# A macaron block on one core: the first feed-forward block's weights quantised by groups of output columns among its first tiles, with ScalarE's sign for part of the groups

## The reference, cut to what matters

```
def _quantize(w):
    gamma = jnp.mean(jnp.abs(w))
    return jnp.clip(jnp.round(w / (gamma + EPS)), -1.0, 1.0)

def _bitlinear(x, w):
    return jnp.matmul(x, _quantize(w).T)

x1 = _bitlinear(x, w1)                 # w1, w2: (1408, 512), w3: (512, 1408)
x2 = _bitlinear(x, w2)
hidden = jax.nn.sigmoid(x1) * x2
return _bitlinear(hidden, w3)
```

## Time and profile before

| | us |
|---|---|
| median of 3 runs | 2888.96 (2887.87 to 2891.6) |
| profiled execution, its span | 2888.6 |
| TensorE busy in the span | 2796.3 (97%) |
| VectorE, ScalarE, GpSimd busy | 2294.6, 1626.3, 1363.4 |

### The profile page before, as it was taken

The page is one execution under the profiler, slowest core; times in us unless marked ns, Lnnn a source line. Parts: engine busy times, 40 slices in busy tenths (PEclk is TensorE's granted clock), DMA queues, the critical chain, the costliest instruction groups (busy, mean ns, idle before and its releaser), DMA issues. The chain is left out here.

```text
span 2888.6 us, 43596 instructions
## 1 busy us (share of the span) xinstructions
PE 2796.3 (97%) x13894; PEld 1952.6 (68%) x13894; DVE 2294.6 (79%) x5940; ACT 1626.3 (56%) x3682; POOL 1363.4 (47%) x2058
## 2 busy tenths in 40 slices
PE   6999899999999999999999999999999999989998
PEld 4888466666666666666666666666666666666887
DVE  7554488989986999988969998888799888984543
ACT  3101476766666776666667666666666667750010
POOL 0000466565654666566546566556456655660000
PEclk8999999999999999999999999999999999999999
DMA  4300311111111121111111211111111111105000
GB/s 171 143 15 15 109 37 37 34 48 35 48 33 58 48 66 34 49 34 49 33 58 48 67 34 48 37 48 30 58 58 57 34 52 36 52 22 193 15 15 30
DMA packets 90835, 151.06 MB, mean 52 GB/s; under 512 B 9200, under 2 KB 30832, under 8 KB 90096
## 3 DMA queue, kind: packets, MB, share of 16 engines
q1 hardware_dynamic: 90608, 148.29, 16.2%
HBM read 127.02 MB, written 21.23 MB: 51 GB/s over the span
## 5 line engine op out<-in xcount | busy, mean ns | idle before, releaser
L750 POOL TENSOR_TENSOR s<-s,tmp 128x256 f32<-128x256 f32 (+1 forms) x448 | 365.0, 815 | 307.3 <-DVE tmp L1043 289.5
L750 POOL TENSOR_TENSOR Y<-aT,D 128x256 f32<-128x256 f32 x384 | 282.2, 756 | 454.0 <-ACT aT L961 454.0
L1425 PEld LDWEIGHTS ps<-Y,S 128*128 128x128 f32 x1536 | 222.2, 192 | 162.8 <-issue 119.3
L750 POOL TENSOR_TENSOR X<-S,D 128x256 f32<-128x256 f32 x384 | 275.9, 718 | 119.0 <-ACT S L912 89.6
L223 ACT ACTIVATE sig<-up_ps 128x512 f32<-128x512 f32 x88 | 52.7, 599 | 451.5 <-PE up_ps L373 451.5
L373 PE MATMUL up_ps<-h_hi,wq 128*128 128x512 f32 x704 | 284.9, 405 | 11.6 <-DVE wq L284 9.7
L373 PE MATMUL up_ps<-h_lo,wq 128*128 128x512 f32 x704 | 280.9, 399 | 0.0
L1413 PEld LDWEIGHTS ps<-AM,XT 128*128 128x128 f32 x1536 | 215.8, 191 | 90.4 <-issue 71.7
L1381 PE MATMUL ps<-hT,slot_w 128*128 128x512 f32 x512 | 261.2, 593 | 5.3 <-DVE tmp L1043 5.3
L1381 PE MATMUL ps<-hT,slot_v 128*128 128x512 f32 x512 | 264.5, 599 | 0.6 <-DVE acc_w L1086 0.6
L1381 PE MATMUL ps<-hT,slot_k 128*128 128x512 f32 x512 | 262.1, 598 | 1.3 <-ACT beta L884 1.3
(11 more groups left out here) (194 smaller groups left out, 6943.0 us busy)
## 6 DMA issues: line engine op xcount, KB each, us to landing
slot_k<-in_wk_dram SPq DMA_DIRECT2D x64, 256.0 KB, 2.6
slot_w<-in_ww_dram SPq DMA_DIRECT2D x64, 256.0 KB, 2.6
slot_q<-in_wq_dram SPq DMA_DIRECT2D x64, 256.0 KB, 2.7
slot_v<-in_wv_dram SPq DMA_DIRECT2D x64, 256.0 KB, 2.7
wo<-in_wo_dram SPq DMA_DIRECT2D x60, 256.0 KB, 3.5
wq_dram<-wq SPq DMA_DIRECT2D x3, 2816.0 KB, 23.5
raw<-in_w_dram SPq DMA_DIRECT2D x8, 704.0 KB, 11.1
x_sb<-in_x_dram SPq DMA_DIRECT2D x4, 1024.0 KB, 6.7
```

The lines of the kernel that those rows point to most:

```text
L750: return nc.gpsimd.tensor_tensor(out, in0, in1, op)
L1425: last = nc.tensor.matmul(pair_columns(bank[f"a2_{l}"], i), ck_(S[l], i), odd_targets(aT, i) if l == 1 else pair_columns(Y[l], i), start=T ...
```

## The change

w1, w2 and w3 are cut into 7 groups of output tiles, `cuts` = 0, 1, 2, 4, 6, 8, 10, 11: a group is all four k-chunks of its tiles for w1 and w2 (four runs of 128 or 256 columns), and its tiles' rows for w3. TensorE waits once per group and matrix. Eight groups, (matrix, group) = (0,0), (0,1), (1,0), (1,1), (0,2), (1,2), (2,0), (2,1), are made with two VectorE passes as before. For the other 13 ScalarE makes sign(raw + gamma/2), in one of two buffers, and VectorE one pass, min(raw > gamma/2, sign). ScalarE's last three magnitude sums come among the sigmoids of tiles 0 and 1, total(2) moves behind the second halves of tiles 0 and 1, and threshold(2) behind hidden(0, 0). down_tile(0, 1) moves one tile later. SyncE loads the rows of block 1 after the third group of w3, those of block 2 after the fifth, the rest and the saves after all.

```diff
--- before.py
+++ after.py
@@ -74,8 +74,10 @@
         if first:
             raw = [sb(f"raw{i}", [P, KT * FF])[:, :] for i in range(2)]
             raw.append(x_sb[:, C:, :].rearrange("p c d -> p (c d)")[:, 0:KT * FF])
-            below = sb("below", [P, FF], BF16)
-            junk = sb("junk", [P, 3 * HID], BF16)
+            below = sb("below", [P, 2 * HID], BF16)
+            both = sb("both", [P, 4 * HID], BF16)
+            signs = [both[:, 0:2 * HID], both[:, 2 * HID:4 * HID]]
+            junk = both
             asum = sb("asum", [P, 3, KT])
             tot = sb("tot", [P, 3])
             gamma = sb("gamma", [P, 3])
@@ -91,10 +93,16 @@
         total_ready = sem("total_ready")
         thr_step = sem("thr_step")
         below_ready = sem("below_ready")
-        quantised = sem("quantised")
+        quantised = [sem(f"quantised{i}") for i in range(3)]
+        signed = sem("signed")
         wq_saved = sem("wq_saved")
         starts = [m for m in (0, 1, 2, 4, 7) if m < MT]
         groups = list(zip(starts, starts[1:] + [MT]))
+        cuts = [0, 1, 2, 4, 6, 8, 10, MT]
+        parts = list(zip(cuts, cuts[1:]))
+        by_sign = [(2, 2), (0, 3), (1, 3), (2, 3), (0, 4), (1, 4), (2, 4), (0, 5), (1, 5), (2, 5),
+                   (0, 6), (1, 6), (2, 6)]
+        by_compare = [(0, 0), (0, 1), (1, 0), (1, 1), (0, 2), (1, 2), (2, 0), (2, 1)]
         normed = [b + 1 for b in range(NB)] if not first else [b for b in range(NB + 1)]
         if not first:
             normed.pop()
@@ -121,6 +129,20 @@
                     turns.append(("rows", b + 1, m - (MT - 4)))
         pair = {turn: i % 2 for i, turn in enumerate(turns)}
+        def part_of(t, i, j):
+            m0, m1 = parts[j]
+            if i < 2:
+                return t[:, :].rearrange("p (k n) -> p k n", k=KT)[:, :, m0 * P:m1 * P]
+            return t[:, m0 * HID:m1 * HID]
+        def small_part(t, i, j):
+            m0, m1 = parts[j]
+            if i < 2:
+                return t[:, 0:(m1 - m0) * HID].rearrange("p (k n) -> p k n", k=KT)
+            return t[:, 0:(m1 - m0) * HID]
         def user_before(turn):
             at = turns.index(turn) - 2
@@ -160,9 +182,13 @@
                 for i in range(3):
                     for k in range(KT):
                         load_raw(i, k)
-                sp.wait_ge(quantised, 3 * KT)
-                for b in range(1, NB):
-                    load_rows(b)
+                sp.wait_ge(quantised[2], 3)
+                load_rows(1)
+                sp.wait_ge(quantised[2], 5)
+                load_rows(2)
+                for i in range(3):
+                    sp.wait_ge(quantised[i], len(parts))
+                load_rows(3)
                 for i in range(3):
                     sp.dma_start(wq_dram[i, :, :], wq[i][:, :].bitcast(FP32)).then_inc(wq_saved, 16)
             else:
@@ -202,26 +228,71 @@
         @block.scalar
         def _(act):
+            def absolutes(i, k):
+                act.wait_ge(raw_full[i][k], 16)
+                if i == 2:
+                    m0, m1 = k * MT // KT, (k + 1) * MT // KT
+                    piece = slice(m0 * HID, m1 * HID)
+                else:
+                    piece = slice(k * FF, (k + 1) * FF)
+                nc.scalar.activation(junk[:, 0:piece.stop - piece.start], raw[i][:, piece], ACT.Abs,
+                                     accum_out=asum[:, i, k:k + 1]).then_inc(abs_summed, 1)
+                act.wait_ge(abs_summed, KT * i + k + 1)
+            def sign(at):
+                i, j = by_sign[at]
+                act.wait_ge(thr_step, 4 * i + 4)
+                if at >= 2:
+                    was, part = by_sign[at - 2]
+                    act.wait_ge(quantised[was], part + 1)
+                nc.scalar.activation(small_part(signs[at % 2], i, j), part_of(raw[i], i, j), ACT.Sign,
+                                     bias=thr[:, i:i + 1]).then_inc(signed, 1)
+            def sigmoid(b, m):
+                n = MT * b + m
+                act.wait_ge(gate_in, n + 1)
+                if n >= 2:
+                    act.wait_ge(hid_step, 3 * (n - 2) + 1)
+                nc.scalar.activation(sig[:, n % 2, :], up_ps[0][pair["tile", b, m]][:, :],
+                                     ACT.Sigmoid).then_inc(sig_ready, 1)
             if first:
-                for i in range(3):
+                for i in range(2):
                     for k in range(KT):
-                        act.wait_ge(raw_full[i][k], 16)
-                        if i == 2:
-                            m0, m1 = k * MT // KT, (k + 1) * MT // KT
-                            piece = slice(m0 * HID, m1 * HID)
-                        else:
-                            piece = slice(k * FF, (k + 1) * FF)
-                        nc.scalar.activation(junk[:, 0:piece.stop - piece.start], raw[i][:, piece], ACT.Abs,
-                                             accum_out=asum[:, i, k:k + 1]).then_inc(abs_summed, 1)
-                        act.wait_ge(abs_summed, KT * i + k + 1)
+                        absolutes(i, k)
+                absolutes(2, 0)
+                sigmoid(0, 0)
+                absolutes(2, 1)
+                sigmoid(0, 1)
+                absolutes(2, 2)
+                absolutes(2, 3)
+                sign(0)
+                sigmoid(0, 2)
+                sign(1)
+                sign(2)
+                sigmoid(0, 3)
+                sign(3)
+                sign(4)
+                sigmoid(0, 4)
+                sign(5)
+                sign(6)
+                sigmoid(0, 5)
+                sign(7)
+                sign(8)
+                sigmoid(0, 6)
+                sign(9)
+                sigmoid(0, 7)
+                sign(10)
+                sigmoid(0, 8)
+                sign(11)
+                sign(12)
             for b in range(NB):
                 for m in range(MT):
-                    n = MT * b + m
-                    act.wait_ge(gate_in, n + 1)
-                    if n >= 2:
-                        act.wait_ge(hid_step, 3 * (n - 2) + 1)
-                    nc.scalar.activation(sig[:, n % 2, :], up_ps[0][pair["tile", b, m]][:, :],
-                                         ACT.Sigmoid).then_inc(sig_ready, 1)
+                    if not (first and b == 0 and m < 9):
+                        sigmoid(b, m)
         @block.vector
         def _(dve):
@@ -274,15 +345,25 @@
                                         ALU.mult).then_inc(thr_step, 1)
                 dve.wait_ge(thr_step, s + 4)
-            def quantise(i, k):
-                piece = slice(k * FF, (k + 1) * FF)
-                dve.wait_ge(quantised, KT * i + k)
-                nc.vector.tensor_scalar(below[:, :], raw[i][:, piece], nthr[:, i:i + 1], None,
-                                        ALU.is_lt).then_inc(below_ready, 1)
-                dve.wait_ge(below_ready, KT * i + k + 1)
-                nc.vector.scalar_tensor_tensor(wq[i][:, piece], raw[i][:, piece], thr[:, i:i + 1],
-                                               below[:, :], ALU.is_gt, ALU.subtract).then_inc(quantised, 1)
+            def quantise(i, j):
+                if (i, j) in by_sign:
+                    at = by_sign.index((i, j))
+                    dve.wait_ge(signed, at + 1)
+                    nc.vector.scalar_tensor_tensor(part_of(wq[i], i, j), part_of(raw[i], i, j), thr[:, i:i + 1],
+                                                   small_part(signs[at % 2], i, j), ALU.is_gt,
+                                                   ALU.min).then_inc(quantised[i], 1)
+                else:
+                    at = by_compare.index((i, j))
+                    if at > 0:
+                        was, part = by_compare[at - 1]
+                        dve.wait_ge(quantised[was], part + 1)
+                    nc.vector.tensor_scalar(small_part(below, i, j), part_of(raw[i], i, j), nthr[:, i:i + 1], None,
+                                            ALU.is_lt).then_inc(below_ready, 1)
+                    dve.wait_ge(below_ready, at + 1)
+                    nc.vector.scalar_tensor_tensor(part_of(wq[i], i, j), part_of(raw[i], i, j), thr[:, i:i + 1],
+                                                   small_part(below, i, j), ALU.is_gt,
+                                                   ALU.subtract).then_inc(quantised[i], 1)
             def hidden(b, m):
@@ -311,17 +392,28 @@
             split_norm(0, 0)
             split_norm(0, 1)
             if first:
-                for i in range(2):
-                    threshold(i)
-                    for k in range(KT):
-                        quantise(i, k)
-                threshold(2)
-                quantise(2, 0)
+                threshold(0)
+                quantise(0, 0)
+                quantise(0, 1)
+                threshold(1)
+                quantise(1, 0)
+                quantise(1, 1)
+                quantise(0, 2)
+                quantise(1, 2)
             for b in range(NB):
                 for m in range(MT):
```

(28 more changed lines are left out.)

## The result

The changed kernel takes 2871.0 us (median of 4 runs, 2869.8 to 2878.7) against 2889.2 us for the kernel before beside it: ratio 0.9942, 95% interval 0.9930 to 0.9954. The 14 runs have a median of 2871.8 and reach from 2868.8 to 2880.7.

What follows compares the result with a forecast made beforehand. Ahead of 47.50 us TensorE was taken to wait for VectorE's wq, behind it to be busy throughout. down_tile(0, 0) at 38.79 against 50.88 gains 12.1 us: 2888.96 - 12.1 = 2876.9 us, range 2874.3 to 2881.2.

Steps and rivals of the forecast that it cites:

- Step 1: First up matmul stays at 22.87 us behind total(1); VectorE's groups take 1.2 us for 512 columns, 2.05 for 1024.
- Step 2: TensorE's four halves of tiles 0 and 1 run without waits, 12 matmuls at 0.43 us, 20 at 0.233, ending at 32.9.
- Step 3: total(2), behind ScalarE's sums and sigmoids, starts at 34.15 us; TensorE waits 1.2 us; up_tile(0, 2) starts at 34.90.
- Step 4: From tile 2, 16 matmuls in 3.73 us plus 0.16: down_tile(0, 0) starts at 38.79 against 50.88, gain 12.1 us.
- Step 5: In the first block's later tiles VectorE keeps 2 to 3 us of slack and ScalarE's signs fit: cost nil.
- Step 6: SyncE's queue: later loads of token-block rows and saves of wq arrive before they are wanted, cost nil.
- The clock was not lost: Rival: the pause at total(2) drops TensorE's clock, 12 matmuls at 0.43 us, 2.4 us given back, 2879.3 us; 18%.
- Table switch: Rival in step 3: ScalarE's table load stalls it 1.4 us longer than 1.29, total 2878.3 us; 4%.
- first half at the high clock: Rival: first half ends at 24.8 us, not 26.04, so ScalarE's chain starts 1.2 us earlier, total 2875.7 us; 5%.
- slower: Rival: VectorE's second pass on columns in four runs is far slower, so TensorE waits for groups, 2895.5 us; 3%.
- no effect: Rival: clock stays low well into the tiles, 60 matmuls 0.2 us dearer eat the 12.1, about 2888 us; 4%.
- theory B: Expectation of the repeat and pause runs: the change shortens the attention for good, 2325.5 within 1 us in every run.

Runs made afterwards that it cites:

- sums_first: Changed kernel with ScalarE's three last magnitude sums ahead of the sigmoids of tiles 0 and 1: 2868.3 us (one run).
- total_early: Changed kernel with total(2) ahead of the second halves of tiles 0 and 1, as before: 2877.8 us (one run).
- filled: Changed kernel with 20 added TensorE matmuls, read by nobody, between total(0) and total(1): 2871.6 us (one run).
- after_third: Changed kernel, nothing changed, run on the same chip as the kernel before beside it: 2870.1 us (5 runs).
- before_third: Kernel before, nothing changed, run on the same chip as the changed kernel beside it: 2889.8 us (11 runs).
- after_again: Changed kernel as it is, run again for a second profile: 2874.8 us (5 runs).
- filled_reordered: Changed kernel with 20 filler matmuls and ScalarE's order sum, sum, sigmoid(0, 0), sum, sigmoid(0, 1), sum: 2867.4 us (5 runs), ratio to before 0.9925.
- grouped_old_order: Changed kernel's groups, two VectorE passes for all, no signs, but in the order of the kernel before: 2888.5 us (one run).
- the padded ones: Changed kernel with 8 or 20 chained VectorE memsets behind the first block's last add: 2882.2 us with 8, 2895.8 us with 20.

## Why the prediction was right, and where it was wrong

**Right: the mechanism in the first block and, within 1.4 us, its size.** The waits for wq are gone, the new bound is total(2) behind ScalarE, VectorE and SyncE cost nothing, and what is gained by tile 2 is kept to the end of the block: 13.51 us at down_tile(0, 0), 13.47 at the last add, against 12.1.

**Step 1, start:** 22.36 in place of 22.87. total(1) came 0.21 earlier, and the other 0.3 was a wrong reading: "right behind total(1)" was not what set 22.87, though the row puts its 0.16 us to issue. The first chunk of wq was ready at 21.09 + 1.68 = 22.77, and the matmul waited for that; with a small group it follows total(1) by 0.45. Groups: 1.27 us for 512 columns (I had 1.2) and 2.07 for 1024 (2.05).

**Step 2, the halves:** 12 matmuls at the low clock, as taken.

**Step 3, the new wait:** total(2) at 33.31 in place of 34.15: the table load is 0.55 earlier with the start, and the sums begin 0.49 behind a sigmoid's start of 0.60 us, so there is an overlap where I had a hand-over. The wait was 0.80, not 1.2; in the other two profiles of this kernel it was 0.71 and 1.58, with total(2) at 33.30 and 33.38. The next matmul stands 0.25 behind total(2), not 0.75: I had copied the 0.75 of total(1), and that one held the wait for wq just named. Together 1.34 us, nearly all of the 1.4 by which down_tile(0, 0) came earlier than in the sum. The switch of table took 1.30 us, 26.20 to 27.50, behind an idle ScalarE, and 1.29 straight behind a sum in sums_first. By the 2.66 of the Trainium skill, ScalarE: Activation LUTs, "What ACT_TABLE_LOAD costs", it would by my estimate have ended 1.4 later; here the trace disagrees with the page of the skill.

**Step 4:** 16 matmuls in 3.81 (33.56 to 37.37), 3.89 taken.

**Step 5, VectorE and ScalarE:** cost nil, as taken. A sign of 1024 columns is 1.15 us where I took 1.06, and without the signs 2.6 us come back. **Step 6:** no wait of the loads or saves reaches an engine that matters.

**The rivals.** Table switch, first half at the high clock, slower, and no effect did not happen. The clock was not lost here, in any of the three profiles of this kernel; behind waits of 5.33 us (total_early) and 1.59 (filled) it was. Its cost there was 2.4 and 1.5 us, near the 2.4 of the rival; that it stayed away in the changed kernel was luck in part, since after_third had a wait as long as that of filled.

**Wrong: the sum carried over, and the range.** The failed step is the sentence that whatever lets TensorE enter its steady stretch earlier "is kept to the end", by which the 12.1 us were taken off 2888.96 with the attention and the last phase unchanged, and in "How the numbers follow" the "1.4 us for the runs' own spread". In the profiles the first block explains 13.5 us; 5.3 us (before_third and after_third) or 6.9 (the first two) more came from the attention and the last phase, whose instructions are the same. The mis-sized first block alone would have given 2875.5, inside the range; the other parts took the median out of it. In those parts the granted clock falls at some places in one execution and not in another, a length at one place differs by 1.1 to 5 us, and in the tail VectorE's passes on `xn` took 2.85 us or up to 3.83. The 1.4 us was smaller even than the scatter of the three runs that it was drawn from, which lay 1.1 below and 2.6 above their median. Some 6 us on both sides would have been the right allowance, as the differences outside the first block show; around 2888.96 less 13.5 that is 2869 to 2882, which holds the medians of all three sets. That margin is worked out after the result.

**Luck or not.** The medians less the last adds of the profiles leave the rest of the program 4.7 us shorter in the changed kernel than in the kernel before in the first set, 1.4 on the chip of after_again and 5.4 on that of after_third, and 5.3 shorter in filled_reordered. The sign is the same four times, so these 1.4 to 5.4 us are not shown to be chance; that the change hands something on that shortens the attention, theory B without its fixed length, stands as a rival. What it hands on can't be the earlier end of the first block (grouped_old_order), and no run says what else it would be.

**Open.** What decides at a given place whether the clock falls isn't settled: the kernel before had the same lengths in two executions, the changed one nearly the same in two of three, and others in the third (after_again, on another chip than after_third; there all five runs took 2873.0 us or more, on that of after_third all five 2871.6 or less). Nothing was run that changes the clock in the attention and nothing else, so that the falls cause the differences is read from matmul counts and granted clocks of equal work, not shown by an edit. The lost clock over the whole attention (the sum over stretches of 3 us of one less the granted clock, times the length) is 17.0 to 17.1 us in four executions, two of each kernel, and does not tell the 4 to 6 us between them apart; in after_again it is 25.6, and there the attention is longer by about as much. My reading, not shown, is that a loss where TensorE has slack costs nothing, and one where it is the bound costs its length; part of the 4 to 6 us is VectorE's 1.9 in the tail, which is no lost clock.

## What to carry to other kernels

Cut weight preparation by the order in which the consumer wants it, and change the order with it: groups alone were 4.6 us slower. Look at what ends a row's wait before copying its delay: the same misread row was wrong by 0.3 us in one step and by 0.5 in another. When TensorE has waits or short matmuls behind the stretch that is changed, don't carry a gain over them unchanged: here the rest of the program moved by up to 11 us from one execution of the same kernel to another. Profile the same kernel twice before explaining a few microseconds. And a stretch made faster ahead of a wait can lose its gain to the clock behind it, as in filled.

## What the runs showed of the hardware

- The same pause of 2.2 us was followed by a granted clock of 0.68 in one kernel and 1.00 in the other, with equal work ahead of it to 0.02 us in that row. At total(2), waits of 0.71 to 0.99 us were not followed by a fall and one of 5.33 was; of five waits of 1.54 to 1.60 us one was (filled) and four were not. So the length of the wait alone did not decide.
- The clock also fell with no wait in the 10 us ahead, during 32 matmuls of 16 columns (after_third, 0.50 from 1442.62 to 1446.62), and stayed at 1.00 at the same place in before_third.
- Four VectorE passes over 512 fp32 columns (`xn`) took 2.85 us in the six profiles in which they began ahead of GpSimd's passes on `Y`, and 3.25 to 3.83 in the eight in which GpSimd had begun 0.14 to 0.19 us earlier.
- The changed kernel's attention took 2325.5, 2327.2 and 2335.3 us in three executions; the three last blocks of tokens without their crossings took 1512.6 in all three.
- Ahead of 27.6 us in the changed kernel the pitch is 0.43, the low clock's, and the clock came back between 25.4 and 28.0 us in its executions and the padded ones without moving total(2) by more than 0.5: ScalarE's chain hid it. In the profile that I quote, the column of the granted clock has 1.00 for this stretch (22.40 to 27.60); there the pitch of the matmuls is to be believed.
